# Decoder layer on one core: gate logic as rows inside the Mamba MLP, mixer and feed-forward unrolled behind it

## The chip, the core and the metric

The kernel runs on one core of a Trainium2 chip. A core has a tensor engine (PE), a vector engine (DVE), a scalar engine (ACT), a general engine (POOL, GpSimd) and a sync engine (SP) that here only issues DMAs. Each runs its own list of instructions in order and they meet through semaphores. The metric is the device time in microseconds; lower is better. A PE matmul in float32 shows as two records in the trace, a transpose as one. PE's clock is granted at one of two levels, 2.4 or 1.2 GHz, shown as 1.00 and 0.50.

## What is computed

Eight batches of 256 tokens with 256 features pass one decoder layer of three parts, each behind a layer norm and with a residual. All in float32.

```python
x = x + attn(layernorm(x))          # Mamba block, then RMS norm and a gated MLP (fc1 to 2 x 1024, fc2)
x = x + xattn(layernorm(x), ctx, ctx)   # mLSTM cell, 4 heads of 64
x = x + ffn(layernorm(x))           # gate/up to 704, down, inputs and weights rounded to FP4 in blocks of 16

# the mLSTM cell
ig = einsum('bsf,hf->bsh', concat([q, k, v]), igate_w) + igate_b      # and fg in the same way
cs = cumsum(log_sigmoid(fg));  log_D = cs - shift(cs).T + ig.T        # lower triangle
m = max(log_D, -1);  C = (q @ k.T / 8) * exp(log_D - m)
h = C / (max(abs(sum(C)), exp(-m)) + 1e-8) @ v;  out = norm_per_head(h) * (1 + out_w)
```

With the running sum `cs`, the running maximum `R` of `ig - cs_shift` is all that the triangle needs: an entry is exp(a[t] - R[s]), with a per-token column `a` and a per-row maximum `R`. The gate stage makes these from the 8 raw gate values of each token.

## The kernel before

The token axis is T = 16 tiles of 128; a batch is C = 2 tiles. The program has two blocks.

The first, `front`, is unrolled by hand over steps k = 0 to 28. Each engine has a list of what it does in step k, and `on(stage, b)` leaves out batches that do not exist. Steps 0 to 17 are layer norm, input projection, convolution and the scan. From step 18 (`MLP`) batch b = k - 18 goes through the gated MLP: `fc1` in four pairs of 128 hidden columns (each pair 8 matmuls of 256 moving columns), `silu_gate` on ACT, `hidden` on DVE; one step later `fc2`, `residual`, statistics and `norm` (the next layer norm, q), and one unit of `quantise` (FP4 rounding of an eighth of the feed-forward weights, 9 DVE steps); two steps later `turn_q`, three steps later `gates`: per 128 tokens four accumulating matmuls with the tokens as stationary and 8 moving columns. `decays`, `mix`, `turn`, `project_out` and `turn_xn` are the rest of the scan, which reaches into steps 18 to 21; `normed` and `turned_xn` on ACT belong to it.

The second block holds `gates(m)` and `mixer_and_ffn(m)`. `gates` takes all batches at once: `softplus_start` and `softplus_finish` on 128x64 values, a transpose to 32 rows of 256, the scans, `R` split in three BF16 pieces and stored to DRAM, and the columns `a_tok` and `nm_tok` by transposes back. In between PE turns the FFN weights (`turn`, 34 transposes) and keeps itself warm (`keep_warm`, 26 and 10 transposes).

Then the mixer runs one batch a slot and the feed-forward one tile a slot. `pipelines` gives each stage a lag in slots, runs the steady part as a hardware loop (`Fori`, two slots a turn), and lets the two overlap for `OVERLAP` = 5 slots from mixer slot `BEGIN` = 7. Mixer: `args` (exponents by rank-3 matmuls and a mask), `exps` on ACT, `scores` q.k (L1438), `weights` on DVE (L1582), `sums` (L1464 to L1466), `normalise` (L1594 to L1611), `squares` on ACT, `variance` (L1616), on POOL the power (L1678), `scale` (L1621), on POOL `residual` (L1683, L1686). `normalise` of batch b waits for the residual of b - 2, as `h` has two buffers. Feed-forward: statistics (L1627, L1632), `norm` on ACT, FP4 rounding of x in 8 DVE steps (lines L318 to L336), `turn_x`, `gate_up` (L1487), `silu`, `product` (L1637), rounding of h, `turn_h`, `down` (L1505), `output` (L1659). The DVE order of a slot is this:

```python
mixer = [(lambda b, p: weights(b, p, 0), 1), (lambda b, p: weights(b, p, 1), 1), (variance, 3),
         (normalise, 2), (scale, 3)]
forward = [(product, 3), *first, (tile_stats, 0), (output, 5), (tile_mean, 0), *last]
pipelines(dve, B, mixer, T, forward, BEGIN, OVERLAP)
```

Other lines in the rows: L923 is `silu_gate`, L683 `turn` of the scan, L717 `fc1`, L730 `fc2`, L740 `turn_q`, L754 and L757 `gates`, L1128 the statistics ahead of `norm`, L272 a reciprocal in the softplus, L1254 a step of the running sums, L1421 the first matmul of `args`.

## Time and profile before

| what | value |
|---|---|
| three runs | 639.83, 641.26, 642.26 us; median 641.26 |
| the profiled execution | 641.21 us, its span 639.5 us, granted clock 0.954 |
| PE busy | 585.2 us, 92% |
| DVE busy | 444.9 us, 70% |
| ACT, POOL busy | 253.8 us, 140.3 us |

The span runs from the first to the last instruction; 1.7 us of the execution lie around it. Busy PE time counts a record's whole pipeline, so "busy" is not "at its peak". The mean over the span hides that stages have different limits, so the profile is read here by windows and by the timeline of an engine: start, duration, engine, line, operation, tiles, and in brackets how long the engine was idle before and what ended that.

### The profile page before, as it was taken

How to read it: one execution, taken by the hardware profiler on the slowest of the kernel's cores; microseconds unless marked ns; L12 is line 12 of the kernel's file. 1: busy time of each engine (PE TensorE's matmuls, PEld its weight loads, DVE VectorE, ACT ScalarE, POOL GpSimd, SP SyncE). 2: the span in 40 equal slices, each digit the busy share in tenths (PEclk: the TensorE clock that was granted, in tenths of full speed). 3: DMA queues.
4: the chain of work that ended last, by engine and by line, in shares of the span. 5: the costliest groups of instructions: out<-in, count | busy, mean ns of one | idle time of the engine just before them, and what ended most of it. 6: DMA issues, size and time to landing. Idle time of an engine off the chain costs nothing. (4 is left out here: it accounts for less than half of the span.)

```text
span 639.5 us, 9652 instructions
## 1 busy us (share of the span) xinstructions
PE 585.2 (92%) x3055; PEld 473.8 (74%) x3055; DVE 444.9 (70%) x968; ACT 253.8 (40%) x546; POOL 140.3 (22%) x192
## 2 busy tenths in 40 slices
PE   7799997899999888999999999889976799999995
PEld 6576664688888777877888888778863477777774
DVE  5895799498974134352444456458898999999994
ACT  2476777744554421111111110164532344444431
POOL 3110000254542111101011001202666322222200
PEclk8799999999999999998999999589986899999998
DMA  9100000000000500000000000134410000000000
GB/s 304 78 1 1 0 14 6 6 6 6 6 3 2 234 1 0 1 2 16 1 17 17 1 17 16 45 90 118 121 46 2 0 10 16 16 16 16 16 18 25
DMA packets 22528, 20.99 MB, mean 33 GB/s; under 512 B 12120, under 2 KB 20696, under 8 KB 22104
## 3 DMA queue, kind: packets, MB, share of 16 engines
q1 hardware_dynamic: 22008, 20.41, 9.8%
q8 instruction: 22, 0.36, 0.3%
q10 hardware_dynamic: 480, 0.07, 0.1%
q14 instruction: 18, 0.15, 0.1%
HBM read 16.04 MB, written 2.34 MB: 29 GB/s over the span
## 5 line engine op out<-in xcount | busy, mean ns | idle before, releaser
L717 PE MATMUL ps<-xnT,w_fc 128*128 128x256 f32 x512 | 114.3, 384 | 0.0
L717 PEld LDWEIGHTS ps<-xnT,w_fc 128*128 128x128 f32 x512 | 97.7, 192 | 13.2
L1487 PE MATMUL ps<-w_fc,scores 128*128 128x352 f32 x256 | 82.9, 479 | 6.1 <-ACT scores L1553 6.1
L1487 PEld LDWEIGHTS ps<-w_fc,scores 128*128 128x128 f32 x256 | 49.1, 197 | 33.8 <-ACT scores L1553 8.1
L1116 DVE TENSOR_TENSOR xs<-ps,xs 128x512 f32<-128x512 f32 x32 | 22.1, 691 | 74.6 <-ACT xs L923 74.6
L923 ACT ACTIVATE xs<-ps 128x512 f32<-128x512 f32 x32 | 19.1, 597 | 108.5 <-PE ps L717 69.9
L730 PE MATMUL ps<-zs,xs 128*128 128x256 f32 x256 | 56.6, 379 | 0.0
L730 PEld LDWEIGHTS ps<-zs,xs 128*128 128x128 f32 x256 | 48.6, 190 | 6.6
L1011 DVE SCALAR_TENSOR_TENSOR fold<-xpad,conv_w,fold 128x256 f32<-128x256 f32 x120 | 50.4, 477 | 0.8
L1505 PE MATMUL ps<-u_res,hT 128*128 128x256 f32 x192 | 45.9, 391 | 3.8 <-DVE scores L1659 2.8
L540 POOL TENSOR_TENSOR bc<-xs,head_c 128x512 f32<-128x512 f32 x16 | 24.9, 1558 | 103.4 <-PE ps L635 76.2
L1505 PEld LDWEIGHTS ps<-u_res,hT 128*128 128x128 f32 x192 | 37.4, 196 | 11.8 <-issue 3.0
L619 PE MATMUL ps<-xnT,fold 128*128 128x256 f32 x160 | 40.2, 400 | 1.7 <-ACT xpad L824 0.9
L619 PEld LDWEIGHTS ps<-xnT,fold 128*128 128x128 f32 x160 | 31.4, 202 | 10.5 <-issue 4.1
L558 POOL TENSOR_SCALAR q_ve<-q_mv 128x2 f32<-128x2 f32 x8 | 1.7, 218 | 144.0 <-DVE q_mv L1132 144.0
L626 PE MATMUL ps<-fold,xnT 128*128 128x512 f32 x64 | 32.9, 639 | 0.0
L692 PE MATMUL ps<-w_out,xF 128*128 128x256 f32 x128 | 30.3, 381 | 0.1
L692 PEld LDWEIGHTS ps<-w_out,xF 128*128 128x128 f32 x128 | 23.7, 190 | 6.4 <-issue 3.8
L1526 ACT ACTIVATE xs<-ps,a_tok 128x256 f32<-128x256 f32 (+1 forms) x64 | 20.8, 436 | 17.8 <-PE ps L1423 17.8
L927 ACT ACTIVATE xnT<-ps 128x512 f32<-128x512 f32 x8 | 4.8, 597 | 52.3 <-PE ps L740 52.3
L1124 DVE TENSOR_TENSOR x_res<-x_res,ps 128x256 f32<-128x256 f32 x16 | 6.7, 420 | 26.6 <-PE ps L730 26.6
L669 PE MATMUL ps<-xpad,fold 128*128 128x64 f32 x192 | 23.3, 274 | 0.0
(260 smaller groups left out, 1172.9 us busy)
## 6 DMA issues: line engine op xcount, KB each, us to landing
xs<-in_ctxT SPq DMA_DIRECT2D x16, 256.0 KB, 3.3
zs<-in_ffn_w SPq DMA_DIRECT2D x1, 2112.0 KB, 9.4
x_res<-in_x SPq DMA_DIRECT2D x8, 256.0 KB, 7.3
w_fc<-in_w_fc SPq DMA_DIRECT2D x1, 2048.0 KB, 10.2
xs<-xnT SPq DMA_DIRECT2D x8, 256.0 KB, 3.4
xs<-in_ctx SPq DMA_DIRECT2D x16, 128.0 KB, 2.7
out<-scores SPq DMA_DIRECT2D x16, 128.0 KB, 1.7
fold<-in_w_in SPq DMA_DIRECT2D x2, 580.0 KB, 6.6
```

Of the source, the lines that this page charges most:

```text
L540: pool.tensor_tensor(heads(dx[:, c, :]), heads(m.xs[:, n, :]), inner(m.head_c[:, 2, :], HD), ALU.mult)\
L619: last = pe.matmul(bank[1 + n % 2][:, 0:S], w_in[:, kk, w0:w0 + P], turned_u(b, kk), start=(kk == 0), stop=(kk == KD - 1))
L626: last = pe.matmul(bank[3 + c][:], turned_u(b, kk)[:, c * P:(c + 1) * P], w_in[:, kk, 0:DI], start=(kk == 0), stop=(kk == KD - 1))
L669: last = pe.matmul(bank[2 + c][:, h * HD:(h + 1) * HD], E[p][c][:, h * P:(h + 1) * P], dtx[:, p, c, h * HD:(h + 1) * HD], start=True, stop ...
L692: last = pe.matmul(bank[6][:, c * D:(c + 1) * D], ygT[:, c, k * P:(k + 1) * P], m.w_out[:, k, :], start=(k == 0), stop=(k == DI // P - 1))
L717: last = pe.matmul(bank[half + r][:, i * S:(i + 1) * S], m.w_fc1[:, kk, col:col + P], m.xnT[:, b, kk * S:(kk + 1) * S], start=(kk == 0), s ...
L730: last = pe.matmul(bank[4 + c][:, 0:D], hid[:, p, k, c * P:(c + 1) * P], w_fc2[:, k, :], start=(k == 0), stop=(k == KM - 1))
L1011: dve.scalar_tensor_tensor(conv[:, p, k, :], xpad[:, p, k, tap:tap + S], m.conv_w[:, ch, tap:tap + 1], conv[:, p, k, :], ALU.mult, ALU.add)\
L1116: dve.tensor_tensor(hid[:, p, 2 * pair:2 * pair + 2, :].rearrange("p k t -> p (k t)"), bank[r][:], gate[:, r, :], ALU.mult).then_inc(g["hi ...
L1487: last = pe.matmul(bank[1 + j][:, 0:HALF], xT[:, p, k * P:(k + 1) * P], m.w_gu[:, k, j * HALF:(j + 1) * HALF], start=(k == 0), stop=(k == ...
L1505: last = pe.matmul(bank[7][:, 0:D], hT[:, p, k, :], m.w_dn[:, k, :], start=(k == 0), stop=(k == KF - 1))
L1526: last = act.activation(w[:, p, i, :], src, ACT.Exp, bias=m.a_tok[:, bass.ds(b * XH + at, 1)])
```

## The change

Both blocks become one, `program`, unrolled on all engines. Steps 0 to 17 stay. From there the work goes in slots; the MLP has 17 (`MLP_SLOTS`), two per batch: in the even slot 2j `fc1` pair 0 of batch j and `fc2` of batch j - 1, in the odd one pairs 1 to 3, `turn_q` and `gates` of batch j - 1.

- Gates as rows: a 48-row output of four matmuls per batch, the gate weights as stationary and the 256 tokens of the batch as moving columns. Four batches accumulate into one bank, each with its weights shifted by 4 rows in zero padding (`gate_pad`).
- The gate chain runs twice, each for four batches as 16 rows of 256, on DVE in slots `CHAIN` = 10 and 18 and the one behind (softplus, then scans and pieces), with its exps on ACT and its transposes (`turn_rows`) on PE. Its stores and loads of the maxima are on SP.
- `quantise` does one unit in each of slots 2 to 9; the FFN weights are turned in nine groups of four transposes in slots 7 to 11 (`turn_weights`).
- Mixer batch b starts in slot 16 + b (`MIX`), its first arguments inside slot 16. It reads q in place (`xnT`) where it was copied by a DMA before. `keep_warm` and the hardware loops are gone.
- The feed-forward starts in slot 22 (`FWD`), mixer slot 6, where it was mixer slot 7. Gate and up weights are laid out in three blocks of 236 + 236 columns, so `gate_up` is three matmuls of 472 per half and not four of 352, and the product takes 708 columns.
- PSUM banks and SBUF tiles are shared out anew, and each reuse has its wait (as `mix_args1(1)` for `gates_read` 2, since both use bank 7).

```diff
--- before.py
+++ after.py
...
+GU = 236
+GU_W = 2 * GU
+ROWS = 16
...
-        together(front)
-        together(gates, mixer_and_ffn)
+        together(program)
...
+    MIX = 2 * B
+    EARLY = 4
+    FWD = MIX + 6
+    SLOTS = FWD + T + 5
+    CHAIN = [10, 18]
...
+        load_gate_k(0)
+        load_gate_k(1)
+        load_k(0)
+        load_v(0)
+        load_v(1)
+        for slot in range(SLOTS):
+            if slot % 2 == 0:
+                on(load_gate_k, slot // 2, n=B if slot >= 4 else 0)
+            if slot == 8:
+                load_k(1)
+            for half in range(2):
+                if slot == CHAIN[half] + 1:
+                    store_max(half)
+            if slot == CHAIN[0] + 1:
+                load_max(0)
+                load_max(1)
+            ahead = slot - MIX - 1 + 2
+            if ahead >= 2:
+                on(load_k, ahead)
+                on(load_v, ahead - 1 if ahead > 2 else B)
+                on(load_max, ahead)
+            on(store, slot - FWD - 5, n=T)
...
-            for half, base in ((0, 0), (2, HM)):
+            for to, base in ((3 * r, 0), (3 * r + 1, HM)):
...
+            for k in range(2 * KD):
+                src = m.xnT[:, b, k * S:(k + 1) * S] if k < KD else kT[:, p, k - KD, :]
+                last = pe.matmul(bank[7][0:3 * ROWS, 0:S], m.gate_pad[:, k, 12 - XH * i:12 - XH * i + 3 * ROWS], src,
+                                 start=(i == 0 and k == 0), stop=(i == EARLY - 1 and k == 2 * KD - 1),
+                                 skip_group_check=True)
+            last.then_inc(g["gates_ps"], 1)
...
+        def turn_weights(n):
+
+            if n == 0:
+                pe.wait_ge(s["xnT_ready"], B)
...
+        def turn_rows(half):
+
+            pe.wait_ge(chain_act[half], 2)
+            if half == 0:
+                pe.wait_ge(g["w_saved"], W_GROUPS)
+            else:
+                pe.wait_ge(x["h_read"], 2)
...
+            if b == 0:
+                pe.wait_ge(g["hid_ready"], PAIRS * B)
+            elif b == 1:
+                pe.wait_ge(g["gates_read"], 2)
...
+            for i in range(3):
                 for k in range(KD):
-                    pe.matmul(to, m.xnT[:, b, k * S + c * P:k * S + (c + 1) * P], m.gate_w[:, k, :],
-                              start=(k == 0), stop=False)
-                for k in range(KD):
-                    last = pe.matmul(to, kT[:, p, k, c * P:(c + 1) * P], m.gate_kv[:, k, :], start=False,
-                                     stop=(k == KD - 1))
-            last.then_inc(g["gates_ps"], 1)
+                    last = pe.matmul(bank[5 + i][:, 0:GU_W], xT[:, t % 2, k * P:(k + 1) * P],
+                                     w_gu[:, k, i * GU_W:(i + 1) * GU_W], start=(k == 0), stop=(k == KD - 1))
...
-            on(fc2, k - MLP - 1)
-            on(turn_q, k - MLP - 2)
-            on(gates, k - MLP - 3)
+        for slot in range(MLP_SLOTS):
+            j = slot // 2
+            if slot % 2 == 0:
+                on(fc1, j, 0)
+                if slot == 0:
+                    turn(B - 1, 0)
+                    turn(B - 1, 1)
+                    project_out(B - 1, 0)
+                    project_out(B - 1, 1)
+                on(turn_xn, j + 4)
+                if slot == MIX:
+                    mix_args0(0)
+                on(fc2, j - 1, 0)
+                on(turn_weights, 2 * (slot - 7), n=W_GROUPS)
+                on(fc2, j - 1, 1)
+                on(turn_weights, 2 * (slot - 7) + 1, n=W_GROUPS)
+                if slot == MIX:
+                    mix_args1(0)
+            else:
+                on(fc1, j, 1)
+                on(turn_weights, 2 * (slot - 7), n=W_GROUPS)
+                on(fc1, j, 2)
+                on(turn_q, j - 1)
+                on(fc1, j, 3)
+                on(turn_weights, 2 * (slot - 7) + 1, n=W_GROUPS)
+                on(gates, j - 1)
+            if slot == CHAIN[0] + 1:
+                turn_rows(0)
+        for slot in range(MLP_SLOTS, SLOTS):
+            if slot == CHAIN[1] + 2:
+                turn_rows(1)
+            on(mix_scores, slot - MIX - 1)
+            if slot == MLP_SLOTS:
+                turn_q(B - 1)
+            on(mix_sums, slot - MIX - 2)
+            on(mix_args0, slot - MIX)
+            if slot == MLP_SLOTS:
+                gates(B - 1)
+            on(mix_args1, slot - MIX)
+            on(turn_in, slot - FWD - 2, n=T)
+            on(turn_out, slot - FWD - 4, n=T)
+            on(gate_up, slot - FWD - 2, n=T)
+            on(down, slot - FWD - 4, n=T)
...
+        for slot in range(MLP_SLOTS):
+            j = slot // 2
+            if slot == 0:
+                turned_xn(3)
+            if slot % 2 == 0:
+                on(silu_gate, j - 1, 3)
+                on(silu_gate, j, 0)
+                if slot == 0:
+                    for c in range(C):
+                        squares(B - 1, c)
+                        turned_y(B - 1, c)
+                on(squares2, j + 5)
+                on(normed, j + 4)
+                on(turned_weights, 2 * (slot - 7), n=W_GROUPS)
+                if slot == CHAIN[0]:
+                    chain_exp(0)
+                on(turned_weights, 2 * (slot - 7) + 1, n=W_GROUPS)
+                if slot == MIX:
+                    mix_exps(0)
+            else:
+                on(silu_gate, j, 1)
+                on(turned_xn, j + 4)
+                on(turned_weights, 2 * (slot - 7), n=W_GROUPS)
+                on(silu_gate, j, 2)
+                on(turned_q, j - 1)
+                on(turned_weights, 2 * (slot - 7) + 1, n=W_GROUPS)
+                if slot == CHAIN[0] + 1:
+                    chain_last_exp(0)
+        for slot in range(MLP_SLOTS, SLOTS):
+            if slot == MLP_SLOTS:
+                turned_q(B - 1)
+            if slot == CHAIN[1]:
+                chain_exp(1)
+            if slot == CHAIN[1] + 1:
+                chain_last_exp(1)
+            on(mix_exps, slot - MIX)
+            on(mix_squares, slot - MIX - 2)
+            on(turned_in, slot - FWD - 2, n=T)
+            on(turned_out, slot - FWD - 4, n=T)
+            on(lift_x, slot - FWD - 1, n=T)
+            on(lift_h, slot - FWD - 3, n=T)
+            on(silu_up, slot - FWD - 2, n=T)
+            on(norm_in, slot - FWD, n=T)
...
+        def chain_start(half):
+            done = chain_dve[half]
+            dve.wait_ge(g["gates_ps"], EARLY * (half + 1))
+            dve.wait_ge(g["x_u"], B)
+            dve.wait_ge(s["xn_ready"], B)
+            if half == 1:
+                dve.wait_ge(g["max_stored"], 16)
+            dve.tensor_scalar(gate_48, bank[7][0:3 * ROWS, 0:S], m.gate_rows[:], None, ALU.add)\
+               .then_inc(g["gates_read"], 1)
+            dve.wait_ge(g["gates_read"], half + 1)
+            softplus_start(dve, done, gate_48[2 * ROWS:, :], lsp, -1.0)
...
-            on(hidden, k - MLP, 0)
-            on(quantise, k - MLP - 1, 0, 3)
-            on(hidden, k - MLP, 1)
-            on(quantise, k - MLP - 1, 3, 5)
...
-            on(hidden, k - MLP, 2)
-            on(quantise, k - MLP - 1, 5, 7)
-            on(hidden, k - MLP, 3)
-            on(quantise, k - MLP - 1, 7, 9)
-            on(residual, k - MLP - 1)
-            on(gate_rows, k - MLP - 3)
-            on(norm, k - MLP - 1)
...
+        for slot in range(MLP_SLOTS):
+            j = slot // 2
+            if slot % 2 == 0:
+                on(sums, j + 6)
+                on(hidden, j - 1, 3)
+                on(quantise, slot - 2, 0, 5)
+                if slot == CHAIN[0]:
+                    chain_start(0)
+                if slot == MIX:
+                    residual(B - 1)
+                on(hidden, j, 0)
+                on(quantise, slot - 2, 5, 9)
+                if slot == CHAIN[0]:
+                    chain_logs(0)
+            else:
+                on(residual, j - 1)
+                on(hidden, j, 1)
+                on(quantise, slot - 2, 0, 3)
+                on(norm, j - 1)
+                if slot == CHAIN[0] + 1:
+                    chain_maxima(0)
+                on(quantise, slot - 2, 3, 6)
+                on(hidden, j, 2)
+                on(quantise, slot - 2, 6, 9)
+                if slot == CHAIN[0] + 1:
+                    chain_columns(0)
+        for slot in range(MLP_SLOTS, SLOTS):
+            if slot == MLP_SLOTS:
+                norm(B - 1)
+            if slot == CHAIN[1]:
+                chain_start(1)
+            if slot == CHAIN[1] + 2:
+                chain_columns(1)
+            on(mix_weights, slot - MIX - 1)
+            on(product, slot - FWD - 3, n=T)
+            on(mix_variance, slot - MIX - 3)
+            if slot == CHAIN[1]:
+                chain_logs(1)
+            on(mix_normalise, slot - MIX - 2)
+            for i in range(5):
+                on(step_x, slot - FWD - 1, i, n=T)
+                on(step_h, slot - FWD - 3, i, n=T)
+            on(mix_scale, slot - MIX - 3)
+            if slot == CHAIN[1] + 1:
+                chain_maxima(1)
+            on(tile_stats, slot - FWD, n=T)
+            on(output, slot - FWD - 5, n=T)
+            on(tile_mean, slot - FWD, n=T)
+            for i in range(6, 9):
+                on(step_x, slot - FWD - 1, i, n=T)
+                on(step_h, slot - FWD - 3, i, n=T)
```

## Rows read from the trace of the kernel before

**Rows 1.** Windows: stretch, length, busy PE, PEld, DVE, ACT, POOL (instructions), clock, DMA, GB/s

```profile
300.00:397.00 97.00, 97.00 (x489) 86.14 (x488) 48.39 (x98) 11.94 (x20) 7.44 (x11) 1.00 0.04 12
397.00:426.00 29.00, 23.23 (x138) 21.97 (x136) 14.79 (x44) 7.99 (x17) 4.43 (x7) 0.71 0.23 66
426.00:506.00 80.00, 65.16 (x414) 52.33 (x412) 66.30 (x146) 33.81 (x86) 40.70 (x44) 0.87 0.22 60
506.00:639.50 133.50, 126.87 (x538) 92.87 (x538) 123.61 (x279) 55.74 (x100) 25.13 (x36) 0.98 0.05 16
```

**Rows 2.** Timeline of PE, one MLP step at its steady pace

```profile
321.02 14.06 PE L717 MATMUL ps<-xnT,w_fc 128*128 128x256 f32 x64
334.92 7.07 PE L730 MATMUL ps<-zs,xs 128*128 128x256 f32 x32
341.83 0.60 PE L740 MATMUL ps<-ident,xs 128*128 128x128 f32 x4
342.26 0.51 PE L754 MATMUL ps<-gate_w,xnT 128*128 128x8 f32 x4
...
343.97 1.33 PE L717 MATMUL ps<-xnT,w_fc 128*128 128x256 f32 x5
```

**Rows 3.** Timeline of ACT and PE, where the MLP begins

```profile
204.69 1.28 ACT L923 ACT_TABLE_LOAD   x1 [2.66 <-PE ps L717]
205.98 0.60 ACT L923 ACTIVATE xs<-ps 128x512 f32<-128x512 f32 x1
...
210.19 0.63 PE L683 MATMUL ps<-ident,zs 128*128 128x128 f32 x4 [1.70 <-ACT xF L894]
```

**Rows 4.** Timeline of all engines, end of the MLP and gate stage

```profile
397.51 0.75 DVE L1128 BATCH_NORM_STATS2 q_st<-x_res 128x6 f32<-128x256 f32 x2
...
400.47 1.11 PE L740 MATMUL ps<-ident,xs 128*128 128x128 f32 x4 [1.33 <-DVE xs L1145]
...
412.90 0.55 DVE L272 RECIPROCAL lsp<-lsp 128x64 f32<-128x64 f32 x1
...
418.54 0.41 DVE L1254 SCALAR_TENSOR_TENSOR aT<-cs,lfT 32x256 f32<-32x256 f32 x1
...
425.58 0.39 PE L1421 MATMUL ps<-rmax,minus_one 128*128 128x512 bf16 x1 [0.50 <-DMA rmax<-running_max]
```

**Rows 5.** Timeline of PE, then of DVE, steady mixer slots

```profile
442.35 2.13 PE L1438 MATMUL ps<-xs 64*128 64x128 f32 x16
...
448.41 2.12 PE L1438 MATMUL ps<-xs 64*128 64x128 f32 x16
...
458.39 1.88 DVE L1582 SCALAR_TENSOR_TENSOR xs<-ps,xs 128x512 f32<-128x512 f32 x3
...
461.33 0.17 DVE L1594 TENSOR_SCALAR den<-ps 128x8 f32<-128x8 f32 x1 [0.47 <-POOL x_res L1686]
...
464.40 0.68 DVE L1621 TENSOR_TENSOR scores<-scores,rv 128x512 f32<-128x512 f32 x1
465.00 1.88 DVE L1582 SCALAR_TENSOR_TENSOR xs<-ps,xs 128x512 f32<-128x512 f32 x3
```

**Rows 6.** Timeline of DVE and PE, joint and steady feed-forward

```profile
478.90 1.01 DVE L320 TENSOR_SCALAR xq_scale<-xq_amax 128x16 f32<-128x16 f32 x1
...
507.75 0.16 DVE L320 TENSOR_SCALAR xq_scale<-xq_amax 128x16 f32<-128x16 f32 x1
...
488.36 6.76 PE L1487 MATMUL ps<-w_fc,scores 128*128 128x352 f32 x16 [3.78 <-ACT scores L1553]
...
506.82 4.97 PE L1487 MATMUL ps<-w_fc,scores 128*128 128x352 f32 x16
...
505.83 0.88 DVE L1637 TENSOR_TENSOR hf<-ps,sg 128x704 f32<-128x704 f32 x1
...
514.26 0.88 DVE L1637 TENSOR_TENSOR hf<-ps,sg 128x704 f32<-128x704 f32 x1
...
522.72 0.88 DVE L1637 TENSOR_TENSOR hf<-ps,sg 128x704 f32<-128x704 f32 x1
```

1077 lines of the change are left out of this document (502 added, 575 removed).

## The prediction, made before the change was run

> **What bounds the kernel now.** I read the windows first [rows 1]. From 300 to 397 us TensorE (PE) is busy for all of 97.0 us, at full clock, while the Vector engine (DVE) is busy for half: in the Mamba MLP any instruction added to PE lengthens the program. From 397 to 426, the gate stage, PE has 23.2 us of work in 29 us, at a mean granted clock of 0.71, and the kernel waits for a chain of small DVE steps, a DMA out and a DMA back. From 426 to 506, the eight mixer batches and the start of the feed-forward, PE is busy 65 of 80 us and DVE 66. From 506 on DVE has 123.6 us of work in 133.5, and until the tail it has no gap: product to product is 8.43 and 8.46 us [rows 6]. So there are three bounds one behind another: PE until 397, a latency chain to 426, then DVE.
>
> **The front, to 200 us.** It stays, except for a few small GpSimd (POOL) writes in `sum_weights`, beside a PE busy throughout. I take 0.
>
> **The MLP.** One batch is fc1 (64 records, 321.02 to 334.92), fc2 (32, to 341.83), turning q (0.43) and gates (342.26 to 343.97, 1.71): 22.95 us [rows 2]. A matmul is two records; with 256 moving columns a record costs 6.91/32 = 0.216 us (334.92 to 341.83). Let T0 be the end of the last fc2, now 397.0, half a us ahead of its statistics at 397.51 [rows 4]; three batches of gates follow it.
> - Gates as rows: four matmuls of 256 columns, 8 records, 8 x 0.216 = 1.73. The old form was 16 records of 8 columns, 1.71. Nothing is won by the form. But gates 0 to 6 now stand ahead of T0, where 0 to 4 did: 7 x 1.73 - 5 x 1.71 = +3.6. A seventh `turn_q` adds 0.4.
> - The 36 transposes of FFN weights move ahead of T0. Of the same size are the four of `turn_q`, from 341.83 to 342.26, 0.11 each [rows 2]: +4.0.
> - `turn_rows(0)` and `mix_args0(0)`: +0.9.
> - Slot 0: only one fc1 pair now stands ahead of `turn(7, .)`. On ScalarE (ACT) the first silu needs a table load of 1.28 us [rows 3], then silu 0.6, and the square and the copy of as many elements are 1.4 more. Before, a second pair of 3.46 us hid most of this and left a wait of 1.70. Worked through, PE gets to the same point 1.4 later: +1.4. The waits for `normed` stay, since fc1, silu and normed stand in the same order.
> - `turn_q(j-1)` behind `norm(j-1)`, which now stands behind `hidden(j, 1)` and three quantise steps: ready at some 7.1 us of a slot, where PE comes at 6.9. 4 x 0.2 = +0.8.
> - First gate chain, slots 10 and 11. Its tiles hold 16 rows of 256, so a step costs what 256 elements cost: 0.41 us [rows 4], with its wait 0.45. The reciprocal is not there at this size; 64 elements took 0.55, and between one plain step (0.45) and four times 0.55 I take 1.45. The logs are then 12 x 0.45 + 1.45 = 6.8 (bounds 5.8 and 7.6), the maxima and pieces ten steps, 4.6. Most lies beside PE. But the exp that starts the logs stands on ACT behind `turned_weights(6)` and needs a table load; DVE then does the logs and only after them `residual(4)` and `norm(4)`, and PE waits for `turn_q(4)`: ready 9.6 us into slot 11, PE there at 7.4. +2.3 (bounds 0 and 5).
> Sum with 0.3 for `turn_weights(0)` behind `turned_xn(7)`: 3.6 + 0.4 + 4.0 + 0.9 + 1.4 + 0.8 + 2.3 + 0.3 = 13.7. T0 moves from 397.0 to 410.7.
>
> At one place a page speaks against the change. The load takes 1.28 us in the row and the silu starts 0.01 us after it [rows 3]. The Trainium skill, ScalarE: Activation LUTs, What ACT_TABLE_LOAD costs, adds a drain of about 1.38 us to every switch to another set. By that rule the four switches of the first chain would cost 2.7 each and T0 would come some 1.4 later; by the row they do not, and the sum goes by the row.
>
> **From T0 to the feed-forward.** I take one mark that both kernels have: the product of FFN tile 1 on DVE, from which both run the same list for 133.7 us. Now it stands at 505.83 [rows 6], T0 + 108.8. Saved is the whole stretch from T0 to the first argument matmul at 425.58 [rows 4], 28.6 us, with its keep-warm transposes, its chain over all batches and its DMA round trip: for batches 0 to 3 all of that is done by T0. What comes instead, in DVE's own order:
> - Slot 17. The last residual ends at T0 + 1.1; from the statistics to the first transpose of q the trace has 2.96 us [rows 4], so `turn_q(7)` is at 4.0, copied at 5.2, argument 0 of batch 1 to 6.0, gates(7) to 7.7. DVE in between does weights(0), 1.9 [rows 5].
> - Slot 18. Second chain: start 7.8 to 9.0. Batch 1 needs bank 7, so arguments and scores come only then, weights(1) ends at 12.4. Logs to 19.2. normalise(0), 3.1 (461.33 to 464.40 [rows 5]), to 22.3. PE waits for it with sums(1): over 4 us idle.
> - Slot 19. weights, variance, 0.6 of waiting, normalise, scale: 29.2. Maxima and pieces: 33.8. ACT's exps of batch 3 stand behind the chain's last exp, PE's `turn_rows(1)` too: PE idle 6 us, then at low clock.
> - Slot 20. Columns 0.5, waits for the scores and sums of that slow stretch 2.7, mixer work 6.3: 43.3.
> - Slots 21 and 22: the loop that bounds the mixer now, in which normalise waits for POOL's residual [rows 5], stays: 458.39 to 465.00, 6.6 a slot. Here 6.7 and, with statistics, 7.3.
> - Slots 23 and 24: mixer 6.3, statistics 0.6, the steps of an x tile 2.9, and 1.4 of DVE's waits beside POOL's residual (the small scale step took 1.01 there and 0.16 alone [rows 6]): 11.2 and 11.3.
> - The joint. ACT's `turned_in(0)` stands behind `mix_squares(6)`, that behind normalise(6). gate_up(0) then runs after an idle PE (6.76 at low clock, 4.97 at full [rows 6]), so product(0) waits: 2.8.
> - Slot 25: an FFN slot without output, 8.1, with variance, normalise and scale of the mixer, 4.4, and 1.4 of waits: 13.9. Then variance and scale of batch 7 in slot 26: 1.9.
> Sum: 43.3 + 6.7 + 7.3 + 11.2 + 11.3 + 2.8 + 13.9 + 1.9 = 98.4 instead of 108.8: -10.4.
>
> **Feed-forward.** Three matmuls of 472 columns a half instead of four of 352: 12 records of 0.40 or 16 of 0.30, 4.8 either way. DVE's list is the same with 708 columns in one step. 0. The outputs' order is the same, and so is the tail.
>
> **Total.** 13.7 - 10.4 = +3.3 on the span of 639.5: 642.8. The profiled execution took 641.21, 1.7 more than its span, and the median of the runs is 641.26, so the two agree. Forecast 644.5, 0.5% slower. The change fills an idle stretch of 29 us but pays for it in PE's full stretch, and runs the gate chain twice, once on the engine that bounds the end.
>
> **Rivals.**
> - DVE saturates behind T0 (faster). Work of DVE between T0 and the mark: residual and norm 2.8, second chain 12.9, mixer 8 x 6.2 = 49.6, statistics 2.4, x steps 8.7, product and h 5.8: 82. If the waits that I counted (16 us) shrink to 6 because other stages fill them, the mark is at T0 + 88: 634. It decides where they fall below 10 us. For it: slots overlap at this joint by design. Against: the trace shows DVE waiting in each mixer slot, on the same POOL residual.
> - The loops themselves cost (faster). A loop turn carries two FFN tiles, so a branch cost would show at every other product. The two distances are 8.43 and 8.46 [rows 6]: no more than 0.03 a turn, under 0.5 in all. [...] If PE's and ACT's turns in the mixer cost 1 us each, some 3 us go: 641.5.
> - It comes out even: the first chain hides (2.3 gone) and product(0) doesn't wait (2.8): 639.4.
> - PE stays at the low clock in slots 19 to 22. A mixer slot is 6.06 us of PE without a gap (442.35 to 448.41 [rows 5]), so at 1.2 GHz it bounds at some 11: 3 or 4 us more in each of two or three slots: 651 to 656.
> - The change doesn't do what it says: the second chain delays all of slots 17 to 20, and the gates might as well stand alone. That is within the forecast; its sign would be a T0 as said with a mark at T0 + 109: 655.
>
> **How the numbers follow.** Forecast (642 to 648) 0.38, somewhat more of it above 644.5 than below; even, with the loops' rival, 0.22; saturated 0.23; low clock or delay 0.17. A measurement tells about 0.5% (3.2 us) from no change: faster is below 638.1, slower above 644.5. Faster 0.27 (saturated, and a part of even), same 0.32, slower 0.41. The range leaves out a tenth at each side: 631 to 654, from a little below the saturated case into the low clock.
>
> **What would show it.** T0 (end of the last fc2 record) at 410.7: below 405 the MLP's additions overlap more than I say. The wait of PE for `turn_q(4)` at 2.3. gates at 1.7 a batch. The second logs 6.8 long ahead of normalise(0). PE idle for over 4 and near 6 us in slots 18 and 19, and a granted clock of one half behind them. The product of tile 1 at T0 + 98.4 and FFN products 8.45 apart. Wrong would make it a DVE without idle time behind T0, or chain steps much cheaper than 0.45.

## The result, and the profile after

The changed kernel takes 654.66 us (median of 4 executions, 652.59 to 658.86); the kernel before took 641.18 beside it. The ratio is 1.022, 95% interval 1.0175 to 1.0265: 2.2% slower, where 644.5 was forecast and 631 to 654 was the range. Two repeats, each beside the kernel before on its chip, gave 1.0226 (1.0174 to 1.0277) and 1.0204 (1.0174 to 1.0234).

The profiled execution took 652.96, with a span of 651.2. T0, the end of the last fc2, is the start of its 32 records plus 32 x 0.216 = 6.91 us: 404.22 + 6.91 = 411.1, against 397.0 before (396.8 by the same sum, as that fc2 starts at 389.86). The second mark, the product of FFN tile 1, is at 514.75, that is T0 + 103.6, against T0 + 108.8. From it to the end the changed kernel takes 136.4 us, the kernel before 133.7.

Windows of the changed kernel, with the columns of [rows 1]: the MLP's end, then by and large slots 17 to 19, slots 20 to 23, the joint, and the feed-forward.

```profile
300.00:411.00 111.00, 109.10 (x518) 90.61 (x517) 44.00 (x98) 25.33 (x43) 4.29 (x10) 0.98 0.04 13
411.00:445.00 34.00, 22.26 (x134) 17.08 (x132) 25.49 (x54) 7.95 (x23) 5.66 (x6) 0.81 0.09 24
445.00:480.00 35.00, 33.33 (x219) 29.02 (x220) 26.56 (x64) 14.97 (x43) 16.03 (x17) 0.80 0.28 70
480.00:515.00 35.00, 20.39 (x70) 11.39 (x70) 30.16 (x64) 10.32 (x20) 16.24 (x19) 0.71 0.00 0
515.00:651.20 136.20, 127.40 (x482) 82.87 (x482) 126.57 (x281) 55.11 (x99) 32.51 (x40) 0.97 0.05 16
```

The idle gate stage is gone, but of its 28.6 us only 5.2 are gained behind T0 (103.6 against 108.8), and T0 itself comes 14.1 later. Between T0 and the mark PE is granted 0.81, 0.80 and 0.71 of its clock, where the gate stage had 0.71 and the mixer slots 0.87 [rows 1], and DVE has 82 us of work in these 104.

PE of the changed kernel in the MLP, with the waits in square brackets; these lines answer to [rows 2, 3]. Four matmuls of gates as rows take 354.93 to 356.79.

```profile
204.26 0.60 PE L785 MATMUL ps<-ident,zs 128*128 128x128 f32 x4
207.83 0.63 PE L785 MATMUL ps<-ident,zs 128*128 128x128 f32 x4 [2.98 <-ACT xF L1176]
208.30 3.62 PE L794 MATMUL ps<-w_out,xF 128*128 128x256 f32 x16
...
293.25 0.66 PE L882 MATMUL ps<-ident,zs 128*128 128x128 f32 x4 [1.47 <-ACT xnT L1197]
...
349.20 0.66 PE L845 MATMUL ps<-ident,xs 128*128 128x128 f32 x4 [1.90 <-DVE xs L1537]
349.69 5.31 PE L823 MATMUL ps<-xnT,w_fc 128*128 128x256 f32 x16
354.93 1.06 PE L859 MATMUL ps<-xnT,gate_pad 128*48 128x256 f32 x4
355.83 1.03 PE L859 MATMUL ps<-xs,gate_pad 128*48 128x256 f32 x4
356.79 0.23 PE L894 MATMUL ps<-ident,u_res 16*128 16x16 f32 x1
...
404.22 7.07 PE L833 MATMUL ps<-zs,xs 128*128 128x256 f32 x32
```

The second gate chain and what it does to PE. All engines of the changed kernel, slots 18 to 20 (the stretch of [rows 5] and of the DVE lines in [rows 4]):

```profile
424.36 1.74 DVE L186 RECIPROCAL u_res<-u_res 16x256 f32<-16x256 f32 x1
...
432.65 0.66 PE L963 MATMUL ps<-xs,u_res 128*128 128x65 f32 x2 [4.10 <-DVE scores L1628]
433.11 0.63 PE L964 MATMUL ps<-xs,u_res 128*128 128x65 f32 x2
...
438.05 0.17 DVE L1617 TENSOR_SCALAR den<-ps 128x8 f32<-128x8 f32 x1 [1.71 <-PE ps L965]
...
441.60 0.67 DVE L1575 TENSOR_TENSOR_SCAN u_res<-u_res 16x256 f32<-16x256 f32 x1
441.76 1.57 POOL L641 TENSOR_TENSOR scores<-scores,out_w 128x512 f32<-128x512 f32 x1 [3.41 <-DVE scores L1644]
442.31 1.30 DVE L1576 SCALAR_TENSOR_TENSOR u_res<-u_res 16x256 f32<-16x256 f32 x1
443.41 1.32 POOL L644 TENSOR_TENSOR x_res<-x_res,scores 128x512 f32<-128x512 f32 x1
443.64 1.37 DVE L1577 TENSOR_TENSOR u_res<-u_res 16x256 f32<-16x256 f32 x1
445.04 0.68 DVE L1578 TENSOR_TENSOR_SCAN u_res<-u_res 16x256 f32<-16x256 f32 x1
...
446.67 0.28 PE L894 MATMUL ps<-ident,u_res 16*128 16x16 f32 x1 [6.53 <-ACT u_res L1231]
...
447.20 3.94 PE L936 MATMUL ps<-xnT,u_res 64*128 64x128 f32 x16
450.40 1.29 DVE L1602 SCALAR_TENSOR_TENSOR u_res<-ps,u_res 128x512 f32<-128x512 f32 x2 [2.07 <-PE ps L936]
456.50 0.17 DVE L1617 TENSOR_SCALAR den<-ps 128x8 f32<-128x8 f32 x1 [3.62 <-PE ps L965]
```

The same kernel in windows of 10 us, with the granted clock in the third column from the right (in the window ahead of these and in the one behind it is 1.00):

```profile
431.00:441.00 10.00, 7.49 (x31) 6.07 (x31) 7.88 (x21) 0.63 (x1) 1.84 (x2) 0.54 0.00 0
441.00:451.00 10.00, 4.33 (x20) 3.96 (x20) 7.58 (x15) 3.35 (x10) 2.89 (x2) 0.50 0.11 30
451.00:461.00 10.00, 10.00 (x49) 8.36 (x49) 5.70 (x14) 3.12 (x9) 2.62 (x3) 0.59 0.33 80
```

PE waits 4.10 and 6.53 us, and behind each wait its matmuls take the time of the lower level: 16 records of scores 3.94 where [rows 5] have 2.13, and a pair of records of the sums 0.43 from start to start where it is 0.22 at full clock. DVE then waits for this PE: 1.71, 2.07 and 3.62.

The joint. PE and DVE of the changed kernel, answering to [rows 6]:

```profile
487.42 0.66 PE L975 MATMUL ps<-ident,scores 128*128 128x128 f32 x2 [5.76 <-DVE e_own L1607]
491.79 7.45 PE L984 MATMUL ps<-fold,scores 128*128 128x472 f32 x12 [3.72 <-ACT scores L1267]
...
500.07 0.90 DVE L1659 TENSOR_TENSOR xF<-ps,xpad 128x708 f32<-128x708 f32 x1 [3.57 <-ACT xpad L1272]
...
514.75 0.88 DVE L1659 TENSOR_TENSOR xF<-ps,xpad 128x708 f32<-128x708 f32 x1
...
521.89 1.95 DVE L247 SCALAR_TENSOR_TENSOR segs<-segs 128x704 f32<-128x704 f32 x1
...
526.04 0.88 DVE L1659 TENSOR_TENSOR xF<-ps,xpad 128x708 f32<-128x708 f32 x1
```

Behind the product of tile 3 the unrolled feed-forward takes 8.43 to 8.46 us from product to product, as the loop did [rows 6].

### The profile page after: what moved, and what is told of

Same layout as the page of the kernel before. It is cut to its first block, busy times and chain, and to the rows that moved or that the text cites. A ratio compares the mean times of both kernels' runs of the same rounds, so it can differ in the third digit from the quotient of the medians.

```text
span 651.2 us, 8655 instructions
## 1 busy us (share of the span) xinstructions
PE 581.9 (89%) x2893; PEld 446.0 (68%) x2893; DVE 458.6 (70%) x983; ACT 258.2 (40%) x552; POOL 144.6 (22%) x196
## 4 chain that ended last, share of the span: by engine, by line
DVE 25%; PE 24%; issue 6%; ACT 1%; POOL 1%; ACTq 0%; DVEq 0%; POOLq 0%
PE ps L823 9%; PE ps L833 5%; DVE segs L233 3%; DVE segs L247 2%; DVE segs L239 2%; DVE segs L249 2%; PE ps L859 2%; PE ps L936 2%; DVE segs L237 1%; PE ps L984 1%; PE ps L1003 1%; DVE segs L241 1%; DVE xF L247 1%; DVE xF L249 1%; PE ps L963 1%
## 5 line engine op out<-in xcount | busy, mean ns | idle before, releaser
L823 PE MATMUL ps<-xnT,w_fc 128*128 128x256 f32 x512 | 117.0, 384 | 0.2 <-DVE bc L1495 0.2
L984 PE MATMUL ps<-fold,scores 128*128 128x472 f32 x192 | 86.3, 603 | 7.6 <-ACT scores L1267 7.6
L984 PEld LDWEIGHTS ps<-fold,scores 128*128 128x128 f32 x192 | 37.7, 203 | 46.2 <-issue 37.2
L1003 PE MATMUL ps<-fold,xpad 128*128 128x256 f32 x192 | 45.9, 390 | 3.7 <-DVE scores L1678 2.8
L1003 PEld LDWEIGHTS ps<-fold,xpad 128*128 128x128 f32 x192 | 37.5, 196 | 14.6 <-issue 8.7
L721 PE MATMUL ps<-xnT,fold 128*128 128x256 f32 x160 | 37.7, 381 | 1.4 <-ACT xpad L1106 0.9
L721 PEld LDWEIGHTS ps<-xnT,fold 128*128 128x128 f32 x160 | 29.7, 191 | 9.4 <-issue 4.1
L1272 ACT ACTIVATE xpad<-ps 128x708 f32<-128x708 f32 x16 | 12.2, 761 | 28.3 <-PE ps L984 28.2
L771 PEld LDWEIGHTS ps<-xpad,fold 128*128 128x128 f32 x192 | 22.5, 192 | 0.1
```

The lines of the kernel that those rows point to most:

```text
L721: last = pe.matmul(bank[1 + n % 2][:, 0:S], w_in[:, kk, w0:w0 + P], turned_u(b, kk), start=(kk == 0), stop=(kk == KD - 1))
L771: last = pe.matmul(bank[2 + c][:, h * HD:(h + 1) * HD], E[p][c][:, h * P:(h + 1) * P], dtx[:, p, c, h * HD:(h + 1) * HD], start=True, stop ...
L823: last = pe.matmul(bank[to][:, i * S:(i + 1) * S], m.w_fc1[:, kk, col:col + P], m.xnT[:, b, kk * S:(kk + 1) * S], start=(kk == 0), stop=(k ...
L984: last = pe.matmul(bank[5 + i][:, 0:GU_W], xT[:, t % 2, k * P:(k + 1) * P], w_gu[:, k, i * GU_W:(i + 1) * GU_W], start=(k == 0), stop=(k = ...
L1003: last = pe.matmul(bank[1][:, 0:D], hT[:, t % 2, k, :], w_dn[:, k, :], start=(k == 0), stop=(k == KF - 1))
```

## The experiments

Each is an edit of the changed kernel, so lines of code are shifted by a few. Ratios are to the kernel before, run beside each. The changed kernel, run again twice, has 654.7 to 656.1 us and ratios of 1.020 to 1.023 in its three series; the kernel before was run again twice too. "The mark" is the product of FFN tile 1, counted from T0 of the same trace, which takes the scatter ahead of T0 out. "The stretch" is the time from fc1(0,0) to the start of the last fc2 in a trace. "A fall" is a time of some us in which PE is granted 0.50 where it had 1.00.

Three single edits (e_warm, e_maxfirst, e_joint) have intervals that overlap with the changed kernel's. What they are worth is read from the mark, in one trace each. In the three traces of the changed kernel the mark is at T0 + 103.5, 103.6 and 104.3. In one kernel whose code behind T0 is the same (e_mlpw) it is at T0 + 105.9, with one more fall some 6 us behind T0.

> The changed kernel itself, as the measure for the runs beside it. Both theories: 653 to 657 us, T0 (end of the last fc2 record) at 411, second logs 6.9 us, product of tile 1 some 103 us behind T0, PE at the low clock from about 432 to 458 us.

656.11 us (651.98 to 657.04). T0 is at 414.6 here, the mark at T0 + 104.3 (103.6 in the first trace). What lies behind T0 repeats within 0.7 us in the three traces of this kernel; the front does not, and that has a section below.

### What the second chain costs

```diff
 def chain_logs(half):
+    if half == 1:  dve.wait_ge(chain_act[half], 1);  return     # no softplus_finish
 def chain_maxima(half):
+    if half == 1:  return
```

> Leaves out the logs, the scans and the pieces of the second gate chain (it reuses the first half's columns for batches 4 to 7), its start, its exps, its transposes and its DMAs stay. Theory 'DVE steps alone': exactly their 6.9 + 6.4 us go, so 641 us. Theory 'starved PE': the two PE waits of 4.1 and 6.5 us go too, and with them the low clock and what DVE waits for it (2.1 + 3.6 us): 635 to 637 us.

The logs, scans and pieces of batches 4 to 7 are left out (these batches then use the columns of the first four), and what waited for these steps waits for the ones that remain. 637.93 us, ratio 0.9933 (0.9899 to 0.9968). The mark is at T0 + 84.4, 19.2 us earlier than in the changed kernel. The steps left out take 6.85 + 6.4 = 13.25 us on DVE. About 6 us more than its own work go with the chain, and PE's granted clock is 1.00 from 411 to 461, where the changed kernel has 0.54, 0.50 and 0.59 from 431 on. That speaks for a PE starved by the chain, but it changes too much at once to show it.

### The clock behind PE's two waits

```diff
+            if slot == CHAIN[1] + 2:                 # ahead of turn_rows(1)
+                pe.wait_ge(x["w_ready"], C * 3);  warm_in(pe, bank[2], m, 60)
+            if slot == CHAIN[1] + 1:                 # ahead of sums(1)
+                pe.wait_ge(x["w1_exp"], 3);  warm_in(pe, bank[7], m, 34)
```

> Adds transposes of the identity on PE in its two waits of slots 19 and 20 (34 and 60, into banks that are free there), nothing else. Theory 'starved PE': the granted clock stays at 1.00 through slots 18 to 21, sums(1), scores(3) and sums(2) take 2.7, 2.1 and 2.7 us again, and 4 to 6 us go: 648 to 651 us. Theory 'DVE steps alone': no change within 1.5 us, 653 to 657.

652.15 us, 1.019 (1.0133 to 1.0247), mark at T0 + 100.8. Behind the first wait the clock stays at 1.00. The 60 transposes of the second end 1.8 us before PE may go on, and slot 20 runs at 0.60 (451 to 461). So the second set was made longer.

> As e_warm, but 82 instead of 60 identity transposes in the second wait of PE, which in e_warm ended 1.8 us before turn_rows(1) and was followed by slot 20 at the low clock (sums 5.1 us instead of 2.7, DVE waiting 3.62 us for them). Theory clock (what the changed kernel loses beyond its chain steps is the low clock behind two waits of PE): slot 20 runs at a granted clock of 1.00, the DVE wait of 3.62 us ahead of normalise(2) falls below 1 us, and the time falls by another 3 to 4 us from e_warm's 652.2 to 648.5. Rival (the clock falls whatever PE did in the wait): slot 20 stays at about 0.6 and the time stays at 652.

647.33 us, 1.0117 (1.0073 to 1.0161), mark at T0 + 97.1. PE and DVE of this kernel:

```profile
436.32 9.12 PE L71 MATMUL ps<-ident 128*128 128x128 f32 x82
445.37 0.23 PE L899 MATMUL ps<-ident,u_res 16*128 16x16 f32 x1
...
445.71 2.13 PE L941 MATMUL ps<-xnT,u_res 64*128 64x128 f32 x16
447.77 0.44 PE L968 MATMUL ps<-xs,w_out 128*128 128x65 f32 x2
...
450.70 0.17 DVE L1627 TENSOR_SCALAR den<-ps 128x8 f32<-128x8 f32 x1 [0.72 <-PE ps L970]
```

No work is saved in this kernel; 116 idle transposes are added. Scores take 2.13 instead of 3.94, DVE's wait of 3.62 is 0.72, and the mark comes 6.5 us earlier (103.6 - 97.1). That is the price of the low clock in slots 19 and 20, and it closes the account of the second chain to within 0.6 us: 97.1 - 84.4 = 12.7 for 13.25 us of DVE work, and 6.5 for the clock.

### POOL beside the maxima

```diff
+            if slot == CHAIN[1] + 1:
+                chain_maxima(1)
             on(mix_scale, slot - MIX - 3)
-            if slot == CHAIN[1] + 1:
-                chain_maxima(1)
```

> chain_maxima(1) stands ahead of mix_scale(0) instead of behind it, so that POOL's residual(0) can't run beside it. Theory contention: the second and third step (1.30 and 1.37 us in the changed kernel) fall to 0.41 and 0.41, maxima and pieces take 4.6 instead of 6.4 us, turn_rows(1) comes 2.4 us earlier, time 2 us less, 652 to 654. Rival (the long steps are long by their own form): they stay at 1.3 and the time changes by less than 1 us.

651.56 us, 1.017 (1.0122 to 1.0217), mark at T0 + 100.6. DVE of this kernel:

```profile
442.95 0.67 DVE L1575 TENSOR_TENSOR_SCAN u_res<-u_res 16x256 f32<-16x256 f32 x1
443.66 0.41 DVE L1576 SCALAR_TENSOR_TENSOR u_res<-u_res 16x256 f32<-16x256 f32 x1
444.11 0.41 DVE L1577 TENSOR_TENSOR u_res<-u_res 16x256 f32<-16x256 f32 x1
```

The same two steps take 0.41 each, so the 1.30 and 1.37 came not from the steps' own form but from POOL's residual beside them. PE's wait ahead of `turn_rows(1)` is 4.09 instead of 6.53, and the mark comes 3.0 us earlier, for a change of order alone. Some of the 3.0 may be a shorter time at the low clock; the run doesn't part the two.

### The logs behind normalise(0)

```diff
-            if slot == CHAIN[1]:
-                chain_logs(1)
             on(mix_normalise, slot - MIX - 2)
+            if slot == CHAIN[1]:
+                chain_logs(1)
```

> chain_logs(1), 6.85 us on DVE, stands behind normalise(0) instead of ahead of it; nothing else changes. Theory DVE sum (the logs cost their 6.85 us wherever they stand, and the turn of the rows waits for the whole chain): PE's wait of 4.1 us ahead of sums(1) goes, its wait ahead of turn_rows(1) grows by 3 to 4 us, weights(3) starts within 1.5 us of T0 + 39.3, time 653 to 656. Rival (the step of the prediction that puts PE's idle time down to normalise(0) behind the logs is where the time goes): the mark comes 4 us earlier, time 650.

656.65 us, 1.0232 (1.0197 to 1.0268), mark at T0 + 104.1. PE's two waits of 4.10 and 6.53 are one of 13.83; weights(3) starts at T0 + 38.9. The mark is where it was, within the scatter of a repeat: the logs cost their length on either side of normalise(0), so the order that the prediction blamed for the first wait is not where the time goes. The rival falls.

### The joint

```diff
+            if slot == FWD + 2:                      # PE, ahead of turn_in(0)
+                pe.wait_ge(x["w0_exp"], B);  pe.wait_ge(x["w1_exp"], B);  warm_in(pe, bank[7], m, 48)
             # ACT, in this slot: turned_in(0) ahead of mix_squares(6)
```

> At the joint alone: ACT's turned_in(0) stands ahead of mix_squares(6) instead of behind it, and 48 identity transposes run on PE in its wait of 5.8 us ahead of turn_in(0). Theory joint (product(0) waits for gate_up(0), which starts late and runs at the low clock): gate_up(0) takes 5.0 instead of 7.45 us and starts 3 us earlier, the DVE wait of 3.57 us ahead of product(0) falls below 0.5, the mark (product(1)) comes at T0 + 100.1 instead of T0 + 103.6, and the time falls by 3.5 us to 651. Rival (it is given back: the next slots wait for POOL or for the exps instead): the wait goes but the mark stays within 1 us of T0 + 103.6, time 654.

650.99 us, 1.0164 (1.0118 to 1.021). PE of this kernel:

```profile
485.52 5.41 PE L71 MATMUL ps<-ident 128*128 128x128 f32 x48
491.49 0.41 PE L980 MATMUL ps<-ident,scores 128*128 128x128 f32 x2 [0.55 <-DVE e_own L1619]
492.37 5.02 PE L989 MATMUL ps<-fold,scores 128*128 128x472 f32 x12 [0.47 <-ACT scores L1276]
```

gate_up(0) takes 5.02 instead of 7.45, the wait for product(0) is gone, and the mark is at T0 + 100.0, 3.6 earlier. Nothing of it is given back. The edit has two parts, ACT's order and the transposes, and no run has one of them alone.

### The weights' transposes in the waits

```diff
-                on(turn_weights, 2 * (slot - 7), n=W_GROUPS)        # and its three like on PE, slots 7 to 11
+            if slot == CHAIN[1] + 1:  ...  turn_weights(0), (1), (2)   # ahead of sums(1)
+            if slot == CHAIN[1] + 2:  ...  turn_weights(3) to (8)      # ahead of turn_rows(1)
```

> Moves the nine groups of weight transposes out of the MLP (slots 7 to 11) into PE's two waits of slots 19 and 20, three groups and six. Both theories agree on the MLP: 36 x 0.11 = 4.0 us and the wait of 1.5 for the last turned_xn go, T0 at 405.6. 'Starved PE': the groups also keep PE a little busy, another 1 to 3 us: 646 to 649. 'DVE steps alone': 5.5 us and no more, 649; if the groups come late they delay turn_rows(1) and give 1 to 2 us back.

647.44 us, 1.0119 (1.008 to 1.0157). From the first fc2 to the last the MLP takes 165.9 us instead of 175.1. Of these 9.2 us, 3.9 are the 36 transposes, 1.47 and 1.90 two waits that they cause (the second, for `turn_q(4)`, because the chain's exp stood behind their copies on ACT), and 1.7 the fall of the clock behind the 1.90 (fc1 5.31 instead of 3.62). But the mark moves to T0 + 105.9, 2.3 later: 12 and 24 transposes do not hold the clock here (0.66 in 421 to 431, 0.51 in 441 to 451), and PE waits for their copies (0.69 us twice) and, behind the 24, another 4.13.

### The front, and its scatter

The first layer's last two turns stand behind one pair of fc1 now, behind two before. This puts the old order back:

```diff
                 if slot == 0:
+                    fc1(0, 1)
                     turn(B - 1, 0)
```

> fc1(0,1) stands ahead of the two last turns of the first layer again, as in the kernel before. My theory: PE's wait for turn(7,1) falls from 2.98 to about 1.6 us, T0 (the end of the last fc2) comes 1.4 us earlier than in a trace with the same clock, and the scatter of T0 among the traces of an unchanged front (411.1 to 416.3 us) goes, because it comes from the granted clock falling behind this wait: T0 at 409.7, time 2 to 3 us below the changed kernel's, 652 to 653. Rival: the fall of the clock comes from the three waits for normed (2.47, 2.47, 1.82), then T0 is 409.7 to 415 as before and the time at most 1.4 us lower.

655.13 us, 1.0211 (1.0178 to 1.0245). The wait is 0.78 instead of 2.98, but the time is that of the changed kernel. Its trace has two falls behind waits for `normed`, at 229 and at 257 us (from slot 2 to slot 4 it takes 28.1 us instead of 26.4), and the stretch is 202.95, only 0.5 less than the 203.5 of the changed kernel. The expected gain is not borne out by this run.

Where a part of the scatter comes from is seen in the repeat of the changed kernel. PE, slot 0 (the changed kernel's own lines are above):

```profile
208.35 1.08 PE L785 MATMUL ps<-ident,zs 128*128 128x128 f32 x4 [2.98 <-ACT xF L1176]
209.23 6.14 PE L794 MATMUL ps<-w_out,xF 128*128 128x256 f32 x16
```

The same 16 records take 6.14 us instead of 3.62. To see whom this belongs to, the kernel before was run again, and the waits for `normed` of slots 2, 4 and 6 were filled.

> The kernel before, once more, for its trace. From fc1(0,0) to the last fc2 it took 188.9 us at full clock. Of eight traces with the changed kernel's order in that stretch, four took 203.3 to 203.5 us and four 206.4 to 206.5, with a granted clock below 1.00 behind the waits for normed. Theory (the fall comes with the waits, which both kernels have): the kernel before shows 188.9 or about 191.9, so the fall is no part of the change. Rival (the change's own order of slot 0 brings it): 188.9 in both repeats.

> As b_again1: a second repeat of the kernel before, 188.9 us from fc1(0,0) to the last fc2 without a fall of the clock, about 191.9 with one.

643.39 and 644.58 us in one execution each. The stretch takes 188.9 and 190.6; behind the first `normed` wait both lose 1.7 us to the clock, and in neither does slot 0 lose anything. The first trace of the kernel before had 188.9 too, but not at full clock, as that expectation has it. It has its own fall, behind a wait ahead of a batch's gates. PE of the kernel before:

```profile
294.61 0.58 PE L754 MATMUL ps<-gate_w,xnT 128*128 128x8 f32 x4 [1.51 <-ACT xnT L915]
...
296.39 15.75 PE L717 MATMUL ps<-xnT,w_fc 128*128 128x256 f32 x64
```

The 64 records take 14.06 at full clock [rows 2]. The second repeat has both falls. Without any, the stretch would be 187.2, and that of the changed kernel 201.8.

```diff
+                if slot in (2, 4, 6):
+                    pe.wait_ge(s["ygT_ready"], T);  pe.wait_ge(s["xnT_ready"], j + 4)
+                    warm_in(pe, bank[5], m, 20 if slot < 6 else 15)
                 on(turn_xn, j + 4)
```

> The changed kernel with 20, 20 and 15 identity transposes in PE's waits for normed, which stand in slots 2, 4 and 6 (e_best3 had its first set in slot 0, where there is no wait, and so paid 2.2 us for it; its set of slot 4 stood in the bank in which the gate rows accumulate). Theory: the granted clock stays at 1.00 behind these waits, the stretch from fc1(0,0) to the last fc2 takes 203.4 us in every trace, and the median is 1 to 2 us below the changed kernel's 654.7 to 656.1. Rival: the scatter arises ahead of slot 0, and the median stays at 655.

653.40 us, 1.0193 (1.016 to 1.0227), a gain of 1 to 3 us that the intervals don't separate from none. No clock is lost behind the filled waits, but slot 0 has its fall (the stretch is 204.8: 201.8 at full clock and 3.0). So both edits were put together and run beside the unchanged kernel.

> The changed kernel with fc1(0,1) ahead of the two last turns (e_slot0) and the transposes in the waits for normed (e_mlpw); everything behind the MLP unchanged. In the traces so far the clock fell behind PE's wait of 2.98 us of slot 0 in five of ten kernels that have it (project_out(7,.) 6.1 us instead of 3.6, 3.0 in all), and in none of eight with the older order. Theory (the order of slot 0 costs 2.2 us plus 3.0 in half of the executions, the normed waits 1.7 in some): the median falls by 3.5 to 4.5 us against a_again2, project_out(7,.) takes 3.6, the stretch from fc1(0,0) to the last fc2 199.6 us. Rival (the front's gain is lost again, as the median of e_slot0, 655.1, suggests): less than 1.5 us.

> The changed kernel once more, beside e_front: 655 us; stretch from fc1(0,0) to the last fc2 203.5 us, or 206.4 with the fall of the clock in slot 0.

652.16 us, 1.0158 (1.0132 to 1.0183), against 654.71 and 1.0204 (1.0174 to 1.0234): 2.6 us, less than the theory's 3.5 to 4.5 and more than the rival's 1.5, and the two intervals overlap a little. The stretch is 199.6, to the number, and without a fall. But the profiled execution is the fastest of the six (648.82 at a mean granted clock of 0.953; the others took 651.45 to 653.27 at 0.945 to 0.948), so falls are likely in the others. Over all twenty traces, the fall that costs 3.0 us in slot 0 is in five of the eleven that have the wait of 2.98, and in none of the nine with the older order (1.70 or 0.78 us). So the change seems to have its part in the scatter; the falls of 1.7 behind the waits for `normed` are older.

Another part lies ahead of all this: fc1(0,0) itself starts between 199.1 and 205.6 us in the twenty traces, at 201.0, 204.3 and 202.6 in those of the kernel before. No edit here touches that, and its cause is open.

### All of it together

```diff
-                on(turn_weights, 2 * (slot - 7), n=W_GROUPS)               # MLP, slots 7 to 11
+                on(turn_weights, 2 * (slot - 8), n=3)                      # slots 8 and 9
+            if slot == CHAIN[1] + 2:  turn_weights(3) to (8);  warm_in(pe, bank[2], m, 42)
+            if slot == CHAIN[1] + 1:  warm_in(pe, bank[7], m, 34)
+                if slot == 0:  fc1(0, 1)                                   # ahead of the two turns
```

> Together: slot 0's order undone; six of the nine groups of weight transposes in PE's second wait (three stay in slots 8 and 9); identity transposes in both waits (34, and 42 behind the six groups). Theory clock and PE-bound MLP: T0 at 401 to 402 (411.1 less 9.2 of e_wmove, plus 1.3 for the three groups, less 1.4), product(1) at T0 + 96 (103.6 less the 4.0 of e_warm and the 3.6 of e_warm2), span 634, time 636, faster than the kernel before by 0.7 per cent. Rival (DVE's own list bounds the mixer, keep-warm gains don't add): product(1) at T0 + 100, time 640, the same as before.

642.80 us, 1.0025 (0.9999 to 1.0051), mark at T0 + 97.2. The mark came near what was said (T0 + 96), T0 did not: 408.7 instead of 401 to 402. Of that, 4.3 us are a front that reached fc1 later in this trace, at 205.0 instead of 200.7, and the rest is about the size of the two falls behind waits for `normed`, at 231 and 259 us, 1.7 each.

The next kernel adds the edits of e_maxfirst and e_joint as they stand above, with 34 transposes in place of the 42.

> e_best with chain_maxima(1) ahead of mix_scale(0) (e_maxfirst) and the joint's order and transposes (e_joint). If the gains add: product(1) at T0 + 91.7 (97.2 in e_best, less 2.0 for the maxima that run alone, less 3.5 at the joint), time 5.5 us below e_best's 642.8: 637.3, ratio 0.994 to the kernel before. Rival (DVE is by now the bound from T0 + 10 on, and only its own work counts): at most 3.5 us of it arrive, 639 to 640, the same as before.

635.47 us, 0.9888 (0.9847 to 0.993), mark at T0 + 90.7. The gains add: 103.6 - 6.5 - 3.0 - 3.6 = 90.5. Here the times bear the marks out: e_maxfirst and e_joint together move the mark by 6.5 us, and the median falls by 7.3, with intervals that are well apart.

The last two add transposes in the MLP's waits, first in slots 0, 2 and 4, then as in e_mlpw.

> e_best2 with 20, 20 and 15 identity transposes in PE's waits for normed in slots 0, 2 and 4 (2.47, 2.47 and 1.82 us). In four of ten traces so far the granted clock fell behind the wait of slot 2 and the stretch from fc1(0,0) to the last fc2 took 3 us more. Theory: that fall is made by the waits; with them filled the stretch has its clean length in every trace, and the median time is 1 to 2 us below e_best2's, 635.6 to 636.3. Rival (the fall comes from elsewhere, or the transposes delay turn_xn): as e_best2 or slower by up to 1 us.

633.29 us, 0.9874 (0.9845 to 0.9903). This kernel does not give the layer's output. Its transposes of slot 4 stand in the bank in which the gate rows of batch 0 already accumulate, which is the likely cause, though no run has that alone; its first set stood where there is no wait. Its successor has them in bank 5 and in slots 2, 4 and 6.

> e_best2 with the transposes of e_mlpw. fc1(0,0) to the last fc2: 193.4 us (203.4 less 9.2 of e_wmove, plus 1.3 for the three groups that stay, less 2.2 of slot 0), where e_best2's trace has 196.7 with a fall of the clock; the mark at T0 + 90.7. Time 632 to 633, ratio 0.986. Rival: as e_best2, 635.5.

631.90 us (629.48 to 633.55), 0.986 (0.9823 to 0.9897): 1.4% faster than the kernel before. It has the change in it, but with fc1(0,1) ahead of the two turns again, six of the nine groups of weight transposes behind the MLP, and idle transposes in PE's waits. The kernel before was not given the like, though it has waits for `normed` and falls of its own, so the 1.4% is not what the change is worth by itself. Its windows: fc1(0,0) to T0, T0 to the mark, the rest.

```profile
200.60:400.80 200.20, 198.66 (x967) 167.18 (x968) 93.71 (x194) 46.25 (x90) 24.32 (x35) 1.00 0.10 33
400.80:491.40 90.60, 79.22 (x559) 63.90 (x557) 79.81 (x179) 36.29 (x94) 37.67 (x42) 0.96 0.14 36
491.40:627.80 136.40, 127.42 (x482) 83.08 (x482) 126.77 (x282) 55.37 (x100) 32.55 (x40) 0.97 0.05 16
```

## Why the prediction missed

The kernel went the way of the fourth rival (PE at the low clock in slots 19 to 22, 651 to 656), which had 0.17 together with delay. The mechanism stood in the prediction; the term for its price was too small. By its own steps:

- **T0**, 410.7 said, 411.1 measured, in part by luck, as misses on both sides cancel. These sizes held: 36 transposes 3.9 (4.0 said), turn_rows and args0 1.0 (0.9), wait for `turn(7, 1)` 1.3 longer (1.4), wait for `turn_q(4)` 1.90 (2.3). The gates cost 1.86 a batch and not 1.73, so their placement 4.5 and not 3.6. The wait of `turn_q(j-1)` (0.8) did not come. The wait ahead of `turn_weights(0)` is 1.47 and not 0.3, but it takes the place of the 1.51 that the kernel before had ahead of its gates, so it adds nothing. What was not in the sum at all is a clock that falls behind PE's waits, 1.7 or 3.0 us each time; here it fell once, behind `turn_q(4)`. So it had in the trace of before, behind that wait of 1.51, and the two falls cancel in the difference of the traces.
- **The table loads.** ACT of the changed kernel in slot 10, where the first chain's exp needs another table:

```profile
336.09 0.66 ACT L1222 ACTIVATE fold<-ps 128x256 f32<-128x256 f32 x2 [3.24 <-PE ps L882]
336.77 1.28 ACT L1227 ACT_TABLE_LOAD   x1
338.06 0.41 ACT L1227 ACTIVATE u_res<-u_res 16x256 f32<-16x256 f32 x1
```

  The load starts 0.02 us behind the copies ahead of it, and the exp 0.01 behind the load, as in [rows 3]. The Trainium skill, ScalarE: Activation LUTs, What ACT_TABLE_LOAD costs, adds a drain of about 1.38 us to a switch; the trace does not agree. The sum was right to go by the row.
- **The logs**, 6.8 said, 6.85 measured, with a reciprocal of 1.74 for the 1.45 estimated. Maxima and pieces: 4.6 said, 6.4 measured. The 1.8 come from the two steps beside POOL (e_maxfirst). The prediction had seen this contention in the x steps and priced it there alone.
- **Slots 19 and 20 are the step that failed**: start of slot 21 at T0 + 43.3 said, T0 + 49.5 measured. PE idle for over 4 and near 6 us was right (4.10, 6.53), and so was the half clock. Wrong was the price: 0.6 and 2.7 us of DVE's waits, 3.3 in all. They were 1.71, 2.07, 3.62 and 0.47, 7.9 in all. With the 1.8 of the maxima these 4.6 make up the 6.2. The prediction let only the scores and sums of slot 20 run slowly. But the clock was low from the end of the first wait to 458, through the sums of slot 19, the second wait and all of slot 20, where one slot is 11.3 us of PE. The rival had that very number (some 11 a slot); it had to stand in the sum. With both waits filled (e_warm2) the mark comes 6.5 us earlier.
- **Slots 21 to 25**: 6.7, 7.3, 11.2, then 14.1 and 13.9 said; 6.8, 7.0, 11.0, 14.7 and 14.7 measured. The wait of product(0) was 3.57 instead of 2.8.
- **Slot 26**: 1.9 said, 2.84 measured (11.29 from the product of tile 1 to the next, where 8.45 is the steady distance). The prediction counted it ahead of the mark, but DVE does the product first in its slot, so it lies behind. Without it the mark was said to be at T0 + 96.5, and it came 7.1 later. DVE's step of 704 elements took 1.95 beside POOL instead of 0.88, once more than I had counted.
- **Feed-forward**: nothing said, nothing measured (116.6 us from the product of tile 3 to the end, 116.8 before). There the loops cost nothing that shows. For the mixer no run has the loops alone; a steady slot takes 6.76 us now (460.61 to 467.37 on DVE) and took 6.6 in the loop [rows 5], so nothing speaks for that rival. DVE does not saturate either: it idles 22 of 104 us.

The sum of the misses is 0.4 + 7.1 + 0.9 = 8.4 us, from a span of 642.8 to one of 651.2. The other 1.7 lie between the profiled execution and the median of the four; I put them down to the scatter ahead of T0, which a single trace can't show. The prediction's range ended at 654, with a tenth of the chance above it. With the waits of slots 19 and 20 at the 7.9 that they took in place of 3.3, the forecast would have been 649; the rival's own price of 3 or 4 us for each of the two slots would have made it 650.5 to 652.5.

What stays open: some 0.9 us of the MLP's lengthening that I could not place; why the clock falls behind a wait of 2.98 us in five of eleven traces only; what moves the start of fc1(0,0) by 6 us; and which of the two edits of e_front brings its 2.6 us, since neither shows alone.
